# A four-layer image block on one Trainium2 core: value rows loaded by image row in the first attention, query copies loaded in four timed pieces and a loop of twelve heads in the last

## The reference

```python
x = x + _L0_conv_ref(_gn(x), ...)   # attention in a 7 x 7 neighbourhood, plus 16 register tokens
x = x + _L1_conv_ref(_gn(x), ...)   # selective scan in four directions
x = x + _L2_conv_ref(_gn(x), ...)   # the same with other weights
x = x + _L3_conv_ref(_gn(x), ...)   # full attention with a relative position bias
```

```python
# L0: 12 heads of 16 channels
scores = jnp.einsum('bnqe,bnke->bnqk', q, k_cat) * scale
scores = jnp.where(mask_cat[None, None], scores, NEG_INF)   # 7 x 7 window, and the registers
attn = jax.nn.softmax(scores, axis=-1)
o = jnp.einsum('bnqk,bnke->bnqe', attn, v_cat)
# L3: 12 heads of 16 channels, all 2304 keys
attn = jnp.einsum('bqd,bkd->bqk', q * scale, k)
attn = jax.nn.softmax(attn + bias, axis=-1)
out = jnp.einsum('bqk,bkd->bqd', attn, v)
```

## Time and profile before

| | us |
|---|---|
| median of 3 runs | 4881.64 |
| lowest, highest | 4876.91, 4882.69 |
| the profiled execution | 4893.03 |
| its span | 4891.2 |
| l0v and the stores behind it, to the first DMA of l0qk | 37.6 to 88.1 |
| l0qk, to the first DMA of the first attention | 88.1 to 223.9 |
| first attention, first to last exponential | 254.6 to 658.2 |
| last attention, first to last exponential | 3391.5 to 4818.3 |

### The profile page before, as it was taken

One profiled execution on the slowest core, in us unless ns is written; L12 is line 12 of the kernel. 1 busy time (PEld: TensorE's weight loads), 2 busy tenths in 40 slices (PEclk: granted clock), 3 DMA queues, 4 the chain that ended last, 5 costly groups with the idle time before them and its releaser, 6 DMA issues. The chain is left out here.

```text
span 4891.2 us, 120325 instructions
## 1 busy us (share of the span) xinstructions
PE 3500.2 (72%) x47313; PEld 1818.4 (37%) x47313; DVE 3579.1 (73%) x3605; ACT 2699.6 (55%) x4416; POOL 1499.8 (31%) x907
## 2 busy tenths in 40 slices
PE   4487855317777766306877765766999999999996
PEld 3266632102222222101222212462665665665563
DVE  4354524869999946687999974456888887888884
ACT  1155524845554532863555542152888888888883
POOL 0011100019999940007999980000000000000000
PEclk8688887558888877656888887856999999999998
DMA  3424321342222220233222221242111111111113
GB/s 87 98 45 69 60 48 34 103 117 60 68 67 60 66 71 15 73 118 83 69 61 65 69 57 39 90 126 65 51 50 50 50 50 50 50 50 50 50 50 87
DMA packets 184511, 320.24 MB, mean 65 GB/s; under 512 B 90011, under 2 KB 129123, under 8 KB 180368
## 3 DMA queue, kind: packets, MB, share of 16 engines
q1 hardware_dynamic: 183952, 312.42, 24.4%
HBM read 203.73 MB, written 108.02 MB: 64 GB/s over the span
## 5 line engine op out<-in xcount | busy, mean ns | idle before, releaser
L1953 DVE TENSOR_REDUCE l3a_mx<-l3a_mx 128x2 f32<-128x768 f32 x1362 | 1231.5, 952 | 287.3 <-PE l3a_mx L1857 282.2
L1929 ACT ACTIVATE l3a_p<-l3a_s 128x384 f32<-128x384 f32 x2592 | 1163.1, 490 | 239.6 <-PE l3a_s L1879 231.1
L1372 POOL TENSOR_TENSOR l_scan_sc<-l_scan_s,l_scan_repc 128x768 f32<-128x768 f32 x576 | 1026.7, 1809 | 5.9 <-DVE l_scan_s L1350 5.7
L1879 PE MATMUL l3a_s<-l3a_q,l3a_k 125*32 125x384 f16 x10368 | 877.6, 331 | 36.5 <-issue 36.1
L1309 ACT ACTIVATE l_scan_da<-l_scan_da,l_scan_a 128x768 f32<-128x768 f32 x576 | 504.0, 875 | 630.7 <-PE l_scan_da L1233 630.7
L1857 PE MATMUL l3a_mx<-l3a_k,l3a_q 124*32 124x384 f16 x10896 | 737.2, 338 | 52.2 <-issue 32.5
L1891 PE MATMUL l3a_o<-l3a_p,l3a_vh 128*32 128x288 f32 x6920 | 608.0, 413 | 20.6 <-ACT l3a_out L1919 18.7
L1233 PE MATMUL l_scan_dup<-l_scan_du,l_scan_pick 96*128 96x512 bf16 (+1 forms) x1152 | 347.4, 390 | 372.0 <-DMA l_scan_dt<-l_dtp 213.7
L1363 POOL TENSOR_TENSOR l_scan_bup<-l_scan_dus,l_scan_repb 128x768 f32<-128x768 f32 x192 | 347.3, 1809 | 654.1 <-DMA l_scan_repc<-l_bcp 654.1
L1823 POOL TENSOR_TENSOR l3a_norm<-l3a_out,l3a_spread 128x576 f32<-128x576 f32 x25 | 35.8, 1433 | 1460.8 <-DMA l3a_spread<-l_inverses 1460.8
L1350 DVE TENSOR_TENSOR_SCAN l_scan_s<-l_scan_da,l_scan_s,l_scan_bu 128x768 f32<-128x768 f32 x256 | 450.6, 1802 | 2.3 <-issue 2.3
(11 more groups left out here) (192 smaller groups left out, 4378.6 us busy)
## 6 DMA issues: line engine op xcount, KB each, us to landing
l3a_q<-l_qx SPq DMA_DIRECT2D x26, 1944.0 KB
l_scan_du<-l_dup SPq DMA_DIRECT2D x144, 144.0 KB, 2.9
l_scan_dt<-l_dtp SPq DMA_DIRECT2D x144, 144.0 KB, 3.4
l_scan_repb<-l_bcp SPq DMA_DIRECT2D x48, 384.0 KB
l_scan_repc<-l_bcp SPq DMA_DIRECT2D x48, 384.0 KB
l3a_q<-l_hx SPq DMA_DIRECT2D x26, 288.0 KB
l_dtp<-l_prep_high_t SPq DMA_DIRECT2D x16, 432.0 KB, 3.1
l_dup<-l_prep_high_u SPq DMA_DIRECT2D x16, 432.0 KB, 3.1
```

The costliest lines, as they stand in the source:

```text
L1372: pool.tensor_tensor(SC[:, st % NSC, :], S[:, n, :], REPC[k % 2][:], ALU.mult).then_inc(weighted, 1)
L1879: mm = pe.matmul(s_ps[g % NS_PS][32 * c:32 * c + 32, 0:SW], K[e % NB][:, keys], Q[e % NB][:, variant(kt * 128 // RG), at:at + SW], start=T ...
L1929: act.activation(P[:, k % NP, third * SW:(third + 1) * SW], s_ps[g % NS_PS][:, 0:SW], ACT.Exp)\
L1953: dve.tensor_reduce(MX[:, h % NB, qt, 2 * pair:2 * pair + 2], mx_ps[bank][:, :, 0:RG], AX_X, ALU.max)\
```

## The change

First attention: a value row keeps the place that its row in the image gives it (image row % 4, image row // 4), whichever window looks at it. So the keys of a window go to `row_place`, the registers to a gap (`regs_place`), and the tile of values in SBUF becomes VC, one copy for each of the three window columns, loaded by 12 DMAs of 22 x 12 x 64 for a group of four heads. POOL builds VH from it by ten instructions for each head. The pair loads move to the start of a pair behind a wait on `scored`, and the shift goes ahead of the output store. The six query masks and six key places are loaded behind `v_projection`'s own loads, then the values are stored, the first image as soon as its tiles are done; the block between is gone.

Last attention: twelve heads in one turn, the queries in four DMAs, each behind a wait on `scored`, the inverses apart from the output, `take_out` one unit earlier, and the first two `values` of a half together behind its second tile.

```diff
-def v_projection(nc, name, XN, wT, bias_dram, V, regs=None):
+def v_projection(nc, name, XN, wT, bias_dram, V, regs=None, behind_loads=None, fill=None):
...
                 sp.wait_ge(loaded, n_loads)
+                if behind_loads is not None:
+                    behind_loads(sp, done)
...
+def row_place(p, r):
+    kr = window_of(p)[1][0]
+    return (kr + r) % 4, (kr + r) // 4 - kr // 4
...
-def load_windows(sp, tile, v_dram, vr_dram, group, strips, sem):
+def load_columns(sp, tile, v_dram, group, slots, sem):
     image = v_dram[group, :, :].rearrange("(h w) e -> h w e", w=W)
-    for strip in strips:
+    for slot in slots:
         for c in range(NPW):
...
+            kc = window_of(c)[1][1]
+            sp.dma_start(tile[32 * slot:32 * slot + KW, c, :, :],
+                         image[slot:H:4, kc:kc + KW, :].rearrange("n w e -> w n e")).then_inc(sem, 16)
...
-                    windows(h + 1, [0])
-                    if h + 3 < NPAIR:
-                        load_pair(sp, h + 3)
-                    windows(h + 1, [1])
+                    columns(h + 1)
                     sp.wait_ge(inverted, h + 1)
...
                 for h in range(NPAIR):
                     if h >= 1:
+                        if h + 2 < NPAIR:
+                            sp.wait_ge(scored, h * IPH)
+                            load_pair(sp, h + 2)
                         normalise(h - 1)
-                    windows(h, [2])
+                    if h + 1 < NPAIR:
+                        load_shift(h + 1)
                     if h >= 1:
                         store_out(h - 1)
-                    if h + 1 < NPAIR:
-                        load_shift(h + 1)
...
-                    for e in range(2):
-                        cols = slice((at + e) * HD, (at + e + 1) * HD)
-                        pool.tensor_copy(VH[h % 2 * 2 + e][:, :, :, 0:HD], VW[g % 2][:, :, :, cols]).then_inc(v_copied, 1)
+                    for home, cols in heads:
+                        for blk in range(4):
+                            pool.tensor_copy(home[:, NPW:NPT - NPW, blk, :].rearrange("p (s c) e -> p c s e", c=NPW),
+                                             vc[:, :, 1 + blk:8 + blk:2, cols]).then_inc(v_copied, 1)
+                        pool.tensor_copy(home[:, 0:NPW, :, :], vc[:, :, 0:4, cols]).then_inc(v_copied, 1)
...
-    HPB = 6
+    HPB = 12
...
+            e, k = (e, x // THIRDS - 1) if x >= THIRDS else (e - 1, KPH - 1)
+            return [] if k % KT == 0 else [(e, k - 1), (e, k)] if k % KT == 1 else [(e, k)]
...
-            e, x = divmod(g - THIRDS // 2 - 1, UPH)
+            e, x = divmod(g - 1, UPH)
...
+    QUERIES_AT, ROWS_AT = (14, 30, 46, 56), 22
...
-                        load_head(sp, (i * HPB + e + 2) % BH, (e + 2) % NB)
+                        load_keys(sp, later, buf)
...
+                        queries(0)
+                        sp.wait_ge(scored, i * ST + (e * UPH + ROWS_AT + LEAD))
+                        load_rows(sp, later, buf)
+                        queries(1)
+                        store_inverses(sp, i * HPB + e, i * HPB + (e + 1))
+                        queries(2)
+                        queries(3)
                         store_out(sp, i * HPB + e, i * HPB + (e + 1))
...
+                    for i in range(3):
+                        for e in range(2):
+                            sp.dma_start(Q[i][3 * HD:QROWS0, e, :], t["l0_qmask"]).then_inc(consts, 16)
+                            sp.dma_start(K[i][3 * HD:QROWS0 + 1, e, :], t["l0_places"]).then_inc(consts, 16)
+                    tiles, parts = L // 128, NH // VG
+                    for b in range(B):
+                        sp.wait_ge(done, (b + 1) * tiles)
```

More of the change, by code:

```diff
@@ L41 @@
 QROWS0 = 3 * HD + KH + KW
-REG_AT = (KH % 4, KH // 4)
+ROWS4 = H // 4
 VG = 4
@@ L363, in _ @@
                 sp.wait_ge(loaded, n_loads)
+                if behind_loads is not None:
+                    behind_loads(sp, done)
+            if fill is not None:
+                @block.gpsimd
+                def _(pool):
+                    fill(pool)
             @block.tensor
@@ L397, in image_of, with regs_place, layer0_attention @@
     return ap.rearrange("p (h w) -> p h w", w=W)
-def load_windows(sp, tile, v_dram, vr_dram, group, strips, sem):
-    part = group % (NH // VG)
+def row_place(p, r):
+    kr = window_of(p)[1][0]
+    return (kr + r) % 4, (kr + r) // 4 - kr // 4
+def regs_place(p):
+    kr = window_of(p)[1][0]
+    return (0, 0) if kr % 4 else (KH % 4, KH // 4)
+def load_columns(sp, tile, v_dram, group, slots, sem):
     image = v_dram[group, :, :].rearrange("(h w) e -> h w e", w=W)
-    for strip in strips:
+    for slot in slots:
         for c in range(NPW):
[L407 to L423, removed]
+            kc = window_of(c)[1][1]
+            sp.dma_start(tile[32 * slot:32 * slot + KW, c, :, :],
+                         image[slot:H:4, kc:kc + KW, :].rearrange("n w e -> w n e")).then_inc(sem, 16)
+COLUMN_LOADS = 16 * 4 * NPW
+def layer0_attention(nc, t, parts_dram, Q, K, VC, RV, v_dram, v_loaded, rv_loaded, consts, eye, o_dram, sum_dram, inv_dram):
     NB = len(Q)
@@ L526, in load_shift, with columns @@
                       .then_inc(shift_loaded, 16)
-                def windows(h, strips):
+                def columns(h):
                     group, odd = (h + 3) // 2, (h + 1) % 2
                     if h >= 1 and group < VGROUPS:
-                        if strips[0] == 0 and not odd:
-                            sp.wait_ge(v_copied, 4 * (group - 1))
-                        load_windows(sp, VW[group % 2], v_dram, vr_dram, group, [3 * odd + x for x in strips], v_loaded[group % 2])
+                        if not odd:
+                            sp.wait_ge(v_copied, 4 * COPIES * (group - 1))
+                        load_columns(sp, VC[group % 2], v_dram, group, [2 * odd, 2 * odd + 1], v_loaded[group % 2])
                 def normalise(h):
@@ L651, in scores @@
                     q = Q[h % NB][:, e, p * PQ:(p + 1) * PQ]
-                    for r in range(KH):
-                        blk, slot = divmod(r, 4)
-                        at = (kr + r) * W + kc
-                        pe.matmul(out[32 * slot:32 * slot + KW, blk, :], k[:, e, at:at + KW], q, start=True, stop=True)
-                    slot, blk = REG_AT
-                    pe.matmul(out[32 * slot:32 * slot + NREG, blk, :], k[:, e, L:LK], q, start=True, stop=True)\
-                      .then_inc(scored, 1)
+                    places = [(*row_place(p, r), slice((kr + r) * W + kc, (kr + r) * W + kc + KW)) for r in range(KH)]
+                    places.append((*regs_place(p), slice(L, LK)))
+                    for slot, blk, keys in sorted(places, key=lambda x: (x[1], x[0])):
+                        n = keys.stop - keys.start
+                        mm = pe.matmul(out[32 * slot:32 * slot + n, blk, :], k[:, e, keys], q, start=True, stop=True)
+                    mm.then_inc(scored, 1)
                 def values(n):
@@ L1761, in store_sums, with store_inverses @@
               .then_inc(sums_loaded, 16)
-        def store_out(sp, row, count):
+        def store_inverses(sp, row, count):
             sp.wait_ge(inverted, count + LEAD)
@@ L1772, in store_out @@
                   .then_inc(inv_spread, 16)
+        def store_out(sp, row, count):
             sp.wait_ge(divided, count + LEAD)
@@ L1781, in _ @@
                 for h in range(2):
-                    load_head(sp, h, h)
+                    load_keys(sp, h, h)
+                    load_rows(sp, h, h)
+                    for v in range(VAR):
+                        load_queries(sp, h, h, v)
                 for i in range(NB):
@@ L2165, in shape_constants @@
     k["l0_qmask"], k["l0_places"] = out_of_reach, places
-    ones = np.zeros((128, 4), np.float32)
-    for r in range(KH):
-        ones[32 * (r % 4):32 * (r % 4) + KW, r // 4] = 1
-    ones[32 * REG_AT[0]:32 * REG_AT[0] + NREG, REG_AT[1]] = 1
+    ones = np.zeros((128, NPT, 4), np.float32)
+    for p in range(NPT):
+        for (slot, blk), n in [(row_place(p, r), KW) for r in range(KH)] + [(regs_place(p), NREG)]:
+            ones[32 * slot:32 * slot + n, p, blk] = 1
     k["l0_ones"] = ones
```

101 lines of the change are left out of this document (57 added, 44 removed).

## The result

| | before | after |
|---|---|---|
| median of the first comparison, us (4 runs each) | 4879.27 | 4719.96 |
| ratio | | 0.9674, 95% interval 0.9657 to 0.9691 |
| the profiled execution | 4893.03 | 4717.87 |
| its span | 4891.2 | 4716.0 |

What follows compares the result with a forecast made beforehand. It blamed store waits in l0qk, and PE's waits for data and late instructions plus low clock in the attentions. Terms 12.7 - 54.9 - 50 - 82 - 10 - 14 = -198 us took 4881.6 to 4683, range 4623 to 4763.

Steps and rivals of the forecast that it cites:

- The place loads on one engine: Before l0qk: six place loads, each on one DMA engine, hold the value stores behind them; +12.7 us, bounds -9 and +17.
- The block l0qk without waits: Block l0qk: slots follow every 8.08 us with no wait for stores, 80.9 us for 135.8; -54.9 us.
- The pacing: Last attention: query loads spread in four pieces stop most stalls from late instruction fetches; -82 us, bounds 0 and -94.
- Rival 1: Last attention: stalls come from the bytes, not their bunching, so pacing does nothing; 4765 us, or 4795; chance 0.09.
- rival 2: Last attention: each of a head's six pieces hits a fetch, so slower if one costs over 1.46 us; chance 0.04.
- rival 3: Both attentions: PE runs without any stall, pairs at 25.4 us and heads at 54.3; 4613 us; chance 0.06.
- the pairs of the first attention: First attention, pairs 1 to 9: DMA waits and some low clock go; -50 us, bounds -94 and -20.
- I keep the issue waits: First attention, pairs 1 to 9: PE's 14.2 us of waits for late instructions stay as they were.
- The other term: First attention, pairs 1 to 9: of 39 us lost to low clock, 27 stay and 12 go.
- the ends of the halves: Last attention: earlier copy of the output saves 0.3 us at each of 48 half ends; -14 us, bounds 0 and -28.
- the turns: Last attention: two of three turns of the loop go, 5 us each; -10 us.
- The base: Whole kernel: the sum of -198 us, taken from the profiled 4893.0, was applied unchanged to the median 4881.6.

Runs made afterwards that it cites:

- the split: Each of the six 37-row place loads sent as 36 rows and one row, against the changed kernel: 4701.5 us for 4718.6.
- the second profile: The changed kernel run and profiled again with nothing altered: median 4718.6 us, 0.9666 of the kernel before.

## Why the prediction was right, and where it was 37 us off

**Right, with its mechanism shown.** The place loads on one engine (+14.9 for +12.7, and the split takes 24.7 us away). One sign of it was missed: the stretch with one engine in sixteen busy stands at 63 to 66 us and not behind 70, since SP itself was held and the stores came only from 65.5. The prediction has no row for the masks' shares in its 42 us (39.6 are the place loads). The changed kernel shows them: there the last three rows of a mask land at 72.3, 72.5 and 72.6 us, one behind the other, while the share is 0.06, and place and mask packets run from 43.3 to 86.3 us, 43.0. The block l0qk without waits (-56.8 for -54.9). The two DMA waits of the first attention, 37.8 us, gone. The pacing (-82 predicted; undone 80 us of L3 span and 88 of the median, done alone 72 and 65), and the late fetches that the prediction named as its reason. Rival 1 fell with that; rival 2 asked for a cost of 1.46 us a piece, and in the last attention 11.9 us over 24 x 6 pieces is 0.08; rival 3 was not reached, since PE still waits 25 us in the first attention and its pairs take 31.2 us there and not 25.4. The twelve engines and 1.6 us that the prediction gives a piece of 108 rows have no row either. In the changed kernel twelve of its 108 packets are on their way at once (median over the middle of a piece), and it takes 2.66 us (median of the 62 pieces that stand alone, 2.15 to 3.27).

**Mis-sized: the pairs of the first attention,** -50 against -41.2 over the nine pairs of the first profile (321.8 to 280.6), -32.6 in the second (289.2), and -33 in the mean of the whole spans. The step that failed is "I keep the issue waits". PE's idle time fell by 29.2 us (54.6 to 25.4) in the first profile and by 27.0 in the second, and not by 37.8, since the issue waits rose by 8: six of the nine pairs had a long one before, and with the key waits of pairs 1 to 3 gone all nine have one. The count itself was short too: the 14.2 us are one line of PE's waits over a longer window, and the nine pairs held 16.8.

The other term was met by luck. In the earlier trace rows 190 matmuls take 9 us at a clock of 0.50 and 185 take 5 us at 1.00, so a low microsecond loses 0.43; the clock of 0.86 makes 90 us low of the 322.6, and 39 us lost. The prediction left 27 of these 39, which at 0.43 is 63 us low. PE's busy time did fall by 12.0 us (267.2 to 255.2) in the first profile, but there the low clock went from 90 us to 45, so each low microsecond that went gave 0.27 and not the 0.43 of the earlier trace rows. In the second profile 64 us were low, as priced, and busy time fell by 5.5 only. Why a low microsecond cost less than in the earlier trace rows stays open.

**Mis-sized: the ends of the halves and the turns.** -14 and -10 predicted. For the ends I named the right danger, that something behind the copy slides, but the wrong engine: it is the maxima that PE waits for, not the exponentials. The turns cost 5 us each as said; by the one profile with six heads, half of what two of them gave went to small stalls within the heads. Together the last attention has -92 for -106, and by the L3 spans the three parts add up to it: 80 for the pacing, 8 for the ends, 4.5 for the turns.

**The base.** The sum was carried from a profiled execution to the median unchanged. The stages give +15 - 57 - 33 - 92 = -167, and the medians -159 in the first comparison, -165 in the second (4883.4 less 4718.6). Of the 37 us, 17 are the first attention and 14 the last; the rest is within the spread of the runs.

## What to carry to other kernels

A stall of the matrix engine that the profile puts down to nothing, a few us behind a burst of large transfers, can be a matter of when the bytes go and not of how many, as in the last attention here (68.3 us of issue waits, and 11.9 with the same loads paced): spread them over the loop with waits on its progress, and then look how long ahead of its use the last piece leaves. In the first attention the same step left the sum of the stalls (24.9 us, then 21.8) and only made them shorter (nine of 1.6 to 3.0 us, then two over 1.3). When a wait is taken away, ask which other wait it hid; here 38 us of waits for data went and 8 us of issue waits came. One profile gives a stage to some 2%; if a sum rests on stages, profile twice.

## What the runs showed of the hardware that was not expected

- Transfers on one DMA engine hold the issuing engine too. Behind three of them SP stands 6.07 to 6.67 us at a further DMA, whatever that one loads: two of the three held were masks. With 36 rows and one the 18 loads were issued in 6 us.
- Nearly the same sum of stalls went with different clocks. 24.9 us of issue waits, nine of them 1.6 to 3.0 us long, go with a clock of 0.92 and nine low stretches; 21.8 us, two of them over 1.3 us, go with 0.96 and three.
- A late fetch of instructions shows in the packets. In the last attention PE went on 1.2 to 2.0 us behind a packet of instructions in each of its 21 long issue waits, and 18 of these packets came 8.0 to 10.7 us behind the last one instead of 5.8.
- In the last attention the issue waits are 68.3 us where the loads are bunched, and 11.9 with the same loads paced. The longest that is left then is the turn of the loop, 3.25 us.
- A fuller body of the loop may not be free: twelve heads had some 15 us of small stalls within the heads, 12 to 21 in the further profiles, six some 10 in the one profile there is.
